# A fused gated cross-attention and ternary feed-forward block on one core: other written orders for the five engines

## The reference, cut to what matters

```python
def attention(x, context, mask, W_q, W_k, W_v, W_o, b_o):
    q, k, v = x @ W_q, context @ W_k, context @ W_v          # split in 8 heads
    sim = where(mask, einsum('bihd,bjhd->bhij', q, k) / 8, max_neg)
    out = einsum('bhij,bjhd->bihd', softmax(sim), v)
    return out @ W_o + b_o

def bitlinear(x, w, b):                                       # both roundings
    return einsum('bsd,fd->bsf', act_quant(rmsnorm(x)), weight_quant(w)) + b

x = x + tanh(g_xattn[0]) * attention(layernorm(x), ctx, mask, ...)
h = gelu(bitlinear(layernorm(x), w1, b1))
x = x + tanh(g_ffn[0]) * bitlinear(h, w2, b2)
```

## Time and profile before

| what | value |
|---|---|
| median of 3 runs | 1108.11 us (1101.25 to 1110.17) |
| the profiled execution | 1108.34 us |
| its span, first to last instruction | 1106.6 us |
| busy share PE, VectorE, ScalarE, POOL | 91%, 77%, 73%, 64% |
| mean granted clock of PE | 0.98 |

### The profile page before, as it was taken

How to read it: one execution, slowest core, us unless ns; L and a number is a source line. 1 busy time by engine, 2 the same in 40 slices (tenths; PEclk the granted TensorE clock), 3 DMA queues, 4 the chain that set the end, 5 groups by cost and what they waited for, 6 DMA issues and landing times.

```text
span 1106.6 us, 26540 instructions
## 1 busy us (share of the span) xinstructions
...
## 2 busy tenths in 40 slices
...
GB/s 236 148 215 214 192 184 144 147 158 148 155 178 113 155 142 170 170 152 161 122 149 143 163 142 159 160 123 168 154 135 150 159 176 131 159 128 131 145 108 29
DMA packets 472335, 169.17 MB, mean 153 GB/s; under 512 B 450320, under 2 KB 452368, under 8 KB 471824
## 3 DMA queue, kind: packets, MB, share of 16 engines
...
## 4 chain that ended last, share of the span: by engine, by line
PE 34%; DVE 13%; DMA 9%; issue 7%; ACT 7%; POOL 6%; SPq 2%; DVEq 0%; POOLq 0%; ACTq 0%
PE ps_g L787 17%; PE ps_g L924 5%; DMA pt<-p 5%; PE ps_g L887 4%; PE ps_g L849 4%; PE ps_s L820 4%; POOL p L1339 4%; DMA hqt<-hq 4%; DVE prob L1007 3%; DVE rrec L948 2%; ACT prob L1182 2%; SPq L751 1%; DVE h_sb L1101 1%; DVE xc L1073 1%; ACT p L1189 1%
## 5 line engine op out<-in xcount | busy, mean ns | idle before, releaser
L1339 POOL TENSOR_TENSOR p<-prob,p 128x750 f16<-128x750 f32 x224 | 356.1, 1602 | 126.4 <-ACT p L1189 124.0
L1007 DVE CUSTOM_DVE_ANT_0 prob<-ps_s,mbias 128x750 f32<-128x750 f32 x224 | 205.0, 933 | 52.5 <-PE ps_s L820 45.5
L787 PE MATMUL ps_g<-ctx,wk 128*128 128x375 f16 x1152 | 202.7, 328 | 30.2 <-POOL ctx L1350 22.6
L1182 ACT ACTIVATE prob<-prob,rmin 128x750 f32<-128x750 f32 x224 | 204.1, 913 | 23.1 <-DVE rmin L1007 22.8
L787 PE MATMUL ps_g<-wv,ctx 128*128 128x512 f16 (+1 forms) x864 | 201.5, 383 | 5.1 <-DVE att L1016 3.1
L787 PEld LDWEIGHTS ps_g<-ctx,wk 128*128 128x128 f16 x1152 | 111.6, 99 | 112.7 <-issue 32.6
L820 PE MATMUL ps_s<-k_sb,q_sb 64*32 64x375 f16 (+2 forms) x2688 | 131.4, 332 | 23.6 <-DVE rmin L1007 22.7
L787 PEld LDWEIGHTS ps_g<-wv,ctx 128*128 128x128 f16 (+1 forms) x864 | 87.8, 104 | 102.7 <-issue 11.1
L849 PE MATMUL ps_g<-pt,v_sb 128*64 128x224 f16 (+2 forms) x2448 | 127.1, 260 | 9.4 <-DMA pt<-p 9.4
L1189 ACT ACTIVATE p<-prob 128x750 f16<-128x750 f32 x144 | 116.7, 820 | 23.9 <-DMA pt<-p 23.2
L849 PEld LDWEIGHTS ps_g<-pt,v_sb 128*64 128x64 f16 x2448 | 113.6, 113 | 10.4 <-issue 8.0
...
## 6 DMA issues: line engine op xcount, KB each, us to landing
...
```

What stands on the lines that cost most here:

```text
L787: mm = nc.tensor.matmul(out, lhs, rhs, start=(m == 0), stop=(m == len(steps) - 1))
L1007: nc.vector.tensor_tensor_reduce(prob[:, (b * NU + n) % PROBS, :].rearrange("p (c k) -> p c k", c=2), ps_s[:, n % 2, :, 0:CH], mbias[:, :] ...
L1182: nc.scalar.activation(prob[:, (b * NU + n) % PROBS, :], prob[:, (b * NU + n) % PROBS, :], ACT.Exp, bias=rmin[:, n:n + 1], scale=-1.0, acc ...
L1339: nc.gpsimd.tensor_tensor(p16[:, u % HILO, 1, 0:J], prob[:, (b * NU + n) % PROBS, :], p16[:, u % HILO, 0, 0:J], ALU.subtract).then_inc(s[" ...
```

## The change

All five tables are written anew. Each holds the same steps as before, once each, in another order; no other line differs. Of PE's 654 steps 413 stand at another place, by 10 places at most; of SyncE's 464 steps 386, by up to 28; of ScalarE's 1023, VectorE's 1026 and POOL's 580 steps 869, 837 and 459. The bank of a result in `ps_g` may change with its turn.

Pieces of the diff: SyncE at the start and in batch 8, PE in batch 0, and the head of POOL's table. The rest is of the same kind.

```diff
 SP_SEQ
-    PD:0:0 LM:0:0 LX:0:0 LC:1:0 LC:0:0 LC:2:0 PD:1:0 WL:0:0 XT:1:0 XT:0:0 PD:2:0 LX:0:1 WL:2:0 WL:1:0 WL:3:0 WL:4:0
-    PD:3:0 LC:0:1 T:0:0 WL:5:0 LC:1:1 T:3:0 XT:0:1 WL:7:0 T:1:0 LC:2:1 T:2:0 XT:1:1 WL:6:0 T:4:0 T:5:0 LX:0:2 BD:0:0
+    PD:0:0 LC:0:0 LX:0:0 LC:1:0 LC:2:0 PD:1:0 LM:0:0 XT:0:0 XT:1:0 WL:0:0 PD:2:0 LM:0:1 LC:0:1 WL:2:0 LX:0:1 WL:1:0
+    WL:3:0 PD:3:0 WL:4:0 T:0:0 WL:7:0 T:1:0 WL:5:0 LC:1:1 T:2:0 WL:6:0 T:3:0 T:4:0 LC:2:1 LX:0:2 XT:1:1 T:5:0 BD:0:0
...
-    XQ:1:7 T:8:8 T:9:8 LR:1:8 F2:1:6 HT:0:7 T:11:8 T:12:8 LM:0:10 T:10:8 LC:1:10 T:13:8 LX:0:11 T:0:9 HT:1:7 XT:1:10
+    T:9:8 LM:0:10 F2:1:6 HT:0:7 LC:0:10 T:10:8 T:12:8 LC:1:10 T:11:8 LX:0:11 XT:0:10 XT:1:10 T:13:8 HT:1:7 LR:1:8
...
 PE_SEQ
...
-    K:7:0 V:4:0 V:5:0 S:3:0 S:4:0 S:5:0 V:0:1 K:0:1 PV:0:0 WM:0:0 S:6:0 V:1:1 V:2:1 Q:0:1 V:3:1 K:1:1 K:2:1 K:3:1
+    V:5:0 K:7:0 Q:3:0 S:3:0 S:4:0 PV:0:0 S:5:0 K:0:1 WM:0:0 V:0:1 V:1:1 V:2:1 K:1:1 S:6:0 K:2:1 V:3:1 K:3:1 K:4:1
...
 POOL_SEQ
...
-    N1:0:0 MB:0:0 CX:0:0 CX:1:0 CX:2:0 L:0:0 H:2:0 N1:0:1 L:1:0 L:2:0 L:3:0 CX:0:1 CX:1:1 L:4:0 H:5:0 H:7:0 L:5:0
+    CX:0:0 N1:0:0 CX:1:0 CX:2:0 MB:0:0 L:0:0 L:1:0 N1:0:1 H:2:0 L:2:0 L:3:0 L:4:0 H:5:0 L:5:0 CX:0:1 CX:1:1 CX:2:1
```

More of the change, by code:

```diff
@@ L84 @@
[L84 to L88, removed]
@@ new lines @@
+    F2:0:9 T:4:11 F2:1:9 LR:1:11 LR:0:11 XQ:1:10 T:5:11 T:6:11 T:7:11 T:8:11 LC:0:13 HT:0:10 T:9:11 LC:1:13 T:11:11
+    T:12:11 T:10:11 T:13:11 HT:1:10 LX:0:14 T:0:12 XT:1:13 LC:2:13 T:1:12 XT:0:13 T:2:12 T:3:12 F2:0:10 XQ:0:11
+    T:4:12 T:5:12 LM:0:13 T:7:12 T:6:12 T:8:12 LR:1:12 XQ:1:11 T:9:12 HT:0:11 LC:0:14 LC:1:14 T:11:12 T:10:12
+    T:13:12 F2:1:10 F2:0:11 T:12:12 LR:0:13 HT:1:11 LC:2:14 LX:0:15 T:0:13 T:1:13 XT:1:14 XT:0:14 T:2:13 T:3:13
+    T:4:13 T:5:13 LR:1:13 XQ:1:12 T:6:13 T:7:13 T:9:13 LM:0:14 T:8:13 LC:1:15 LC:0:15 LM:0:15 T:11:13 T:10:13
@@ new lines @@
+    F1:7:3 S:0:5 PV:1:4 K:4:5 K:5:5 S:1:5 F2:0:3 V:4:5 V:5:5 K:6:5 K:7:5 PV:2:4 PV:3:4 S:2:5 Q:2:5 Q:3:5 F2:1:3
+    S:3:5 O:1:4 S:4:5 V:0:6 V:1:6 Q:0:6 Q:1:6 K:0:6 S:5:5 K:1:6 PV:0:5 S:6:5 K:2:6 V:2:6 V:3:6 K:3:6 V:4:6 K:4:6
+    S:0:6 PV:1:5 F1:4:4 F1:5:4 F1:6:4 K:5:6 F1:7:4 K:6:6 Q:2:6 V:5:6 PV:2:5 S:1:6 K:7:6 PV:3:5 S:2:6 Q:3:6 O:0:5
+    O:1:5 S:3:6 F2:1:4 S:4:6 Q:0:7 F1:0:5 V:0:7 F1:1:5 F1:2:5 F1:3:5 K:0:7 Q:1:7 K:1:7 S:5:6 PV:0:6 S:6:6 V:1:7
+    V:2:7 V:3:7 K:2:7 K:3:7 K:4:7 S:0:7 PV:1:6 F1:4:5 F1:5:5 F1:6:5 F1:7:5 V:4:7 V:5:7 F2:0:5 K:5:7 K:6:7 S:1:7
@@ L215 @@
[L215 to L217 removed]
+    PW:0:0 CX:0:0 CX:1:0 XH:0:0 CX:2:0 XH:1:0 PW:1:0 K:0:0 K:1:0 K:2:0 Q:0:0 K:3:0 Q:1:0 WA:0:0 Q:2:0 PW:2:0 E:0:0
+    K:4:0 H:0:0 E:1:0 E:2:0 K:5:0 H:1:0 WA:1:0 V:0:0 E:3:0 E:4:0 E:5:0 WA:2:0 V:1:0 H:3:0 H:4:0 V:2:0 V:3:0 V:4:0
@@ new lines @@
+    F1:6:10 F1:7:10 R:3:11 M:0:12 KL:5:12 M:1:12 VL:4:12 VL:5:12 GM:1:10 G2:1:10 F2:0:10 KL:6:12 M:2:12 M:3:12
+    XH:0:13 XH:1:13 KL:7:12 QL:2:12 PA:2:11 PA:3:11 M:4:12 QL:3:12 M:5:12 M:6:12 M:7:12 R:0:12 O:0:11 L2:0:11
+    F2:1:10 O:1:11 L3:0:11 M:8:12 M:9:12 QL:0:13 QL:1:13 L2:1:11 VL:0:13 F1:0:11 KL:0:13 F1:1:11 F1:2:11 F1:3:11
+    L3:1:11 M:10:12 M:11:12 N1:0:14 PA:0:12 R:1:12 VL:1:13 VL:2:13 GM:0:11 KL:1:13 KL:2:13 G2:0:11 VL:3:13 M:12:12
+    M:13:12 XN:0:14 PA:1:12 KL:3:13 KL:4:13 F1:4:11 F1:5:11 F1:6:11 F1:7:11 R:2:12 M:0:13 M:1:13 VL:4:13 F2:0:11
@@ L327 @@
+    L:8:14 H:10:14 L:9:14 PL:0:14 G2:0:13 L3:1:13 L:10:14 MB:0:15 H:12:14 PL:1:14 L:11:14 L:12:14 L:13:14 L:0:15
+    L:1:15 H:2:15 L:2:15 XB:1:14 G2:1:13 PL:2:14 L:3:15 L:4:15 PL:3:14 H:5:15 L:5:15 H:7:15 L2:0:14 PL:0:15 L2:1:14
+    L:6:15 L:7:15 L:8:15 L:9:15 L3:0:14 PL:1:15 PL:2:15 G2:0:14 XB:0:15 H:10:15 L:10:15 H:12:15 PL:3:15 L:11:15
+    L:12:15 L:13:15 PL:4:15 PL:5:15 G2:1:14 PL:6:15 PL:7:15 L2:0:15 XB:1:15 L2:1:15 L3:1:14 G2:0:15 L3:0:15 L3:1:15
+    G2:1:15
 """)
```

441 lines of the change are left out of this document (212 added, 229 removed).

## The result

| | before | after |
|---|---|---|
| median (range) | 1109.14 us (1101.25 to 1112.35) | 1071.02 us (1070.68 to 1074.54) |
| ratio to before, 95% interval | | 0.967 [0.962, 0.973] |
| span of the profiled execution | 1106.6 us | 1069.1 us |
| PE busy / idle | 1006.2 / 100.4 us | 995.9 / 73.2 us |
| time at half clock, stretches | 46.8 us, 10 | 22.7 us, 7 |

Of the 37.5 us of span, 27.2 are idle time of PE and 10.3 are busy time, with the same 9856 matmuls: PE was at half clock for 24.1 us less. Half of that, 12, is the estimate for a PE that works through all of it; the 10.3 us measured agree with it.

What follows compares the result with a forecast made beforehand. It took PE's matmuls to set the pace, with gains only where PE idles or runs slow; start 3, batch 0 3, turnings 7, other waits 0 and tail 2 make 15 us off 1108, so 1093 us, range 1078 to 1110.

Steps and rivals of the forecast that it cites:

- the turnings: SyncE's order of turnings: finished ones no longer held behind unmade ones, 7 us less, bounds 0 and 18.5.
- the start: Before PE's first matmul: fewer POOL steps ahead of it, so PE starts 3 us earlier, bounds 0.8 to 4.
- waits for row minima: PE's waits for VectorE ahead of score units: 3 us less in batch 0 and 2 us in the tail.
- batch 0: Fifth and sixth score units: the first weighing set between them hides row minimum waits, 3 us, bounds 0 and 6.
- tail: After 1000 us: other work covers the row minimum wait ahead of `S:6:15`, 2 us, bounds 0 and 4.
- waits for `pt`: PE's waits for turnings of the probabilities: 5 us of 9.4 go.
- waits for `hqt`: PE's waits for turnings of `hq`: only 1 us of 7.4 goes, as the distance hardly grows.
- all other waits: Remaining waits for row minima, `ps_g` banks and loads: no net change, bounds 6 us either way.
- PE's busy time (less half clock): One drop of PE's clock to half avoided with the turning waits: 1.7 us.
- (A): POOL holds VectorE: each further bad meeting costs up to 7 us, with three 1114 us; chance 0.15.
- (B): PE's waits only change places; only the start and part of the tail are gained, 1104 us; chance 0.32.
- (C): ACT and POOL, no longer held by turnings, bring row minima earlier too: 1080 us; chance 0.13.

Runs made afterwards that it cites:

- head_old: Changed kernel, but the steps the kernel before had started by 125 us keep the old order: 1083.3 us, ratio 0.979.
- late_new: Kernel before up to 550 us, the new order of all engines from there: 1094.1 us, ratio 0.989.
- after_sorted: Changed kernel with its 38 turnings that stood behind a later one sorted on SyncE by POOL's low halves: 1069.5 us, ratio 0.966.
- before_sorted: Kernel before with only SyncE's 224 turnings sorted into the order of POOL's low halves: 1092.8 us, ratio 0.989.
- head_195: New order of all engines for what starts by 195 us, then the old order with turnings sorted: 1079.7 us, ratio 0.977.
- late_before: Kernel before with two tiny unused loads ahead of each of the 224 turnings on SyncE: 1245.5 us, ratio 1.127.
- b_f2: before_sorted with nine F2 products that waited for `hqt` put one step later on PE: 1116.6 us, ratio 1.008.

## Why the prediction was wrong

Its direction was right; the sum was too small, above all in the term for the turnings. By the two profiled executions (37.5 us of span), against the terms of the sum:

| | forecast | measured |
|---|---|---|
| the start | 3 | 6.2 |
| waits for row minima (batch 0: 3, tail: 2) | 5 | 7.3 |
| waits for `pt` | 5 | 7.0 |
| waits for `hqt` | 1 | 7.1 |
| all other waits | 0 | -0.4 |
| PE's busy time (less half clock) | 1.7 | 10.3 |

The forecast column adds up to 15.7, which the prediction rounded down to 15. Of the 22 us that are missing, 8.6 are the clock, 6.1 the waits for `hqt` and 3.2 the start.

**The start**, 3 us with bounds 0.8 to 4: measured 6.2. The mechanism was right, and the mask bias was hidden as said. What failed was the choice of a duration: "5.13 / 2 + 3.65 = 6.2 us, or 2 x 3.65 = 7.3 us if both are as slow as the third" took the roundings at the lengths of the earlier trace rows; the two took 3.57 together. Also the mark "first matmul at 19 to 20" was missed, at 16.45. Why they were longer before was not tried.

**Batch 0**, 3 us, bounds 0 and 6: the wait of 3.78 ahead of the sixth unit is gone, as said, and 2.00 ahead of the fifth stands, with 1.34 new ahead of a product of Q. The lead goes from 6.2 at the first matmul to 8.0 at `S:6:0`, so the term was 1.8. But it then grows to 13.8 by batch 2, where "all other waits" were taken at 0 with bounds of 6. This part of the gain is placed, not explained (by PE's waits it is small pieces, and one wait of 4.50 us for VectorE's low half of a product of V is new): the weights' preparation, the first turnings and the first score units all moved there.

**The turnings**, 7 us, bounds 0 and 18.5. Here stood the steps that failed. "Of the 9.4 us for `pt` I take 5 off" was near: 7.0. Of the 7.4 us for `hqt` it took 1, since "the distance hardly grows"; 7.1 went, so that distance, counted in PE's matmuls, does not say whether the landing comes in time. And "one clock drop of 1.7 us" was far too few: five in the middle stage became one, ten in all became seven, and PE's busy time fell by 10.3 us. The direct waits and the clock, wherever it fell, are 24.4 us against the 7.7 that the term was made of, and above its upper bound of 18.5, which allowed for one clock drop only.

The waits of ACT and POOL for turnings were put at nothing: "no row, since PE is mostly ahead of neither". They fell from 47.5 to 14.1 us, but for PE they show little: in the middle stage of the new kernel the row minimum costs as much as before (10.3 us against 9.7). Sorting alone did come with 5.1 us fewer waits for row minima, 2.8 of them in the middle stage, and this is the most that the runs allow for that link. The step "room comes mostly from SyncE's order" was right for what sorting can give: sorted, the old order gains 16.8 us between batches 1 and 15, the new one 18.8. It does not hold for `hqt`, whose waits sorting left at 7.8 us; they go only where the new order of all engines stands (head_old 0.3, late_new 1.5). The count that stood beside it, 52 turnings behind a later one against 38, undersold it, since it does not tell how long each was held; by the issue rows and the low halves, the turnings stood 760 us in all on SyncE after they were made before, and 605 sorted, 580 in the new kernel. (Nor is that sum a price: 529 us in after_sorted brought no time.)

**The tail**, 2 us, bounds 0 and 4: 3 measured alone, 2.6 by the lead. `S:6:15` has no wait, as said.

```profile
1011.66 1.13 PE L820 MATMUL ps_s<-k_sb,q_sb 64*128 64x375 f16 x12
1013.81 0.30 PE L837 MATMUL ps_g<-ident,rrec 128*64 128x128 f16 x4 [1.02 <-DVE rrec L951]
...
1018.19 3.32 PE L887 MATMUL ps_g<-w,xqt 128*128 128x512 fp8e4 x8 [3.06 <-DVE h_sb L1101]
...
1033.81 4.40 PE L787 MATMUL ps_g<-wo,attn 128*128 128x512 f16 x12 [2.24 <-POOL attn L1345]
```

"The other wait keeps its surroundings" was not so: the 2.02 us for the last turning are gone, and a product of the feed-forward part waits 3.06 in other company.

The marks for right in the profile were met but for the first matmul's time: PE's waits for `pt` are 2.4 us (below 5), `T:10:8` goes out 1.1 us after its low half, and no wait above 2 us stands ahead of the two named score units. Of the marks for wrong none came. But the 2.0 us wait ahead of `S:4:0` and a half-clock stretch behind it (from 55.1) stayed.

**The rivals.** (A), POOL holding VectorE, asked what further bad meetings would cost. What came is its reverse: the kernel before had two behind which PE waited and its clock fell, and the new one is rid of both. One is in the earlier trace rows, 3.56 us of wait and 6.8 us of half clock. The other is the 6.25 us scaling, with POOL busy throughout, and PE's next wait behind it:

```profile
334.73 6.25 DVE L948 TENSOR_SCALAR rrec<-rrec 128x4 f16<-128x4 f32 x1
...
337.79 3.16 POOL L1339 TENSOR_TENSOR p<-prob,p 128x750 f16<-128x750 f32 x2
...
341.54 1.46 PE L787 MATMUL ps_g<-wv,ctx 128*128 128x512 f16 x3 [3.11 <-DVE att L1016]
```

The clock fell there for 3.4 us. Together 3.11 + 1.7 + 3.56 + 3.4 = 11.8 us, an estimate of what the two had cost, and the new kernel's lead jumps by 4.4 us between batches 4 and 5 and by 5.5 between 9 and 10, where they stood. Both stay in the splices and edits that keep the old order at that place (before_sorted: 6.26 and 3.64 us long, PE waits 3.12 and 3.44; head_195: 3.12 and 3.50), though not in late_before, where the added loads shift everything. Neither comes back where the new order stands. So about 10 of the 21 us of the middle fit meetings that went away. The prediction had read both in the earlier trace rows as a risk of the new order and never as a cost that it might remove, so no term of the sum holds them; no run took a meeting away alone. The two lines read after

```profile
L948 DVE TENSOR_SCALAR rrec<-rrec x67: 169/318/1610, 46.3 to 1024.8; 128x4 f16<-128x4 f32 x45, 128x2 f16<-128x2 f32 x22
...
L1073 DVE TENSOR_SCALAR xc<-xr,mv x28: 485/488/1793, 122.6 to 1040.0; 128x512 f32<-128x512 f32 x28
```

The worst of each fell from 6.25 and 3.64 us to 1.61 and 1.79. One new bad meeting did come, on another line, with three low halves of POOL beginning at 590.09; PE waited 1.69 us behind it and the clock did not fall:

```profile
590.59 4.70 DVE L1051 SCALAR_TENSOR_TENSOR xh<-xa,rs,xh 112x512 f16<-112x512 f32 x1
...
596.00 2.15 PE L787 MATMUL ps_g<-wv,ctx 128*110 128x512 f16 x9 [1.69 <-DVE h_sb L1101]
```

Over five lines of short VectorE instructions (L948, L951, L1047, L1051, L1073) the time above about the shortest of each line is 91.9 us before and 88.1 after: the new order has as much of it, and less of it where PE waits. The rule of the Trainium skill that the prediction set beside this rival ("SBUF — State Buffer", "Who interferes with whom"), that whichever of the two starts first holds a shared pair of ports for its whole instruction while the other blocks, agrees with that in kind; no run here separates the ports from other causes. (B), the waits only change places, is false for the change and true for b_f2, which is what it looks like. (C), the chains loosen as a whole, with 1080 us, came nearest in time, and late landings went as it says. Its own link, row minima that come earlier because ACT and POOL are not held, is not shown: outside the head and the tail they were waited for as before.

**Adding up.** By the lead: 14 us up to batch 2, 21 in the middle, 2.6 in the tail. By the runs: head and sorting together give 25 us (head_195), the tail 3, and 6 remain between it and the new kernel (1079.7 - 3 - 1071.0, with 5 us of uncertainty in the first alone). head_195 keeps the two meetings of rival (A), whose waits alone are 6.6 us, and the new kernel does not; they would fill this gap, but no run changed them alone. A larger ring of `p16` was not tried; nor was the new order of turnings alone in the old kernel, where some would wait for what stands behind them.
